# Router selection by pairwise ranks, and a new order of five pieces in the opening of a cross-attention and mixture-of-experts kernel

## What is computed

```python
def xattn(q, k, Wq, Wk, Wv, Wo):            # q = layernorm(x), k = ctx
    sim = einsum('bqd,bkd->bqk', q @ Wq.T, k @ Wk.T)
    sim = (sim - mean(sim, (1, 2))) * rsqrt(var(sim, (1, 2)) + EPS)
    return einsum('bqk,bkd->bqd', softmax(sim), k @ Wv.T) @ Wo.T

def ffn(x):                                 # x = layernorm(x)
    shared = swiglu(x @ sw1 + sb1) @ sw2 + sb2
    probs = softmax(x @ gate_w + gate_b)    # 8 experts
    topk_probs, topk_idx = top_k(probs, 2)
    cw = sum(one_hot(topk_idx, 8) * topk_probs[..., None], axis=2)
    routed = einsum('ebsd,bse->bsd', swiglu(x @ rw1 + rb1) @ rw2 + rb2, cw)
    return shared + routed

x = x + xattn(layernorm(x), ctx, ...)       # x: (8, 256, 128), ctx: (8, 256, 96)
x = x + ffn(layernorm(x), ...)
```

## Time and profile before

| | us |
|---|---|
| median of 3 runs | 155.4 |
| lowest and highest | 154.41, 155.75 |
| the profiled execution | 152.72 |
| its span, first to last instruction | 150.7 |
| TensorE busy | 132.1 (88%) |
| VectorE busy | 108.1 (72%) |
| ScalarE busy | 70.6 (47%) |
| GpSimd busy | 23.7 (16%) |

### The profile page before, as it was taken

The page is one execution under the profiler, slowest core; times in us unless marked ns, Lnnn a source line. Parts: engine busy times, 40 slices in busy tenths (PEclk is TensorE's granted clock), DMA queues, the critical chain, the costliest instruction groups (busy, mean ns, idle before and its releaser), DMA issues.

```text
span 150.7 us, 2018 instructions
## 1 busy us (share of the span) xinstructions
PE 132.1 (88%) x603; PEld 96.5 (64%) x603; DVE 108.1 (72%) x337; ACT 70.6 (47%) x132; POOL 23.7 (16%) x41
## 2 busy tenths in 40 slices
PE   0998894498999999499999998899899989999980
PEld 0786681486878766368778775667576656766740
DVE  3676968486886988974966988829986883865641
ACT  2347955666133127973353129962133783313320
POOL 7083366304020001040200000000300000000000
PEclk9999997558999999999999999999999999999999
DMA  4999000000000000009510000049020008720002
GB/s 127 298 340 255 6 0 7 0 0 2 0 0 4 0 0 2 0 23 325 213 66 8 0 0 0 5 148 382 33 70 0 0 4 229 327 70 7 0 0 72
DMA packets 8493, 11.38 MB, mean 76 GB/s; under 512 B 1265, under 2 KB 6922, under 8 KB 8098
## 3 DMA queue, kind: packets, MB, share of 16 engines
q1 hardware_dynamic: 7906, 11.02, 21.9%
q10 hardware_dynamic: 576, 0.23, 0.6%
HBM read 10.15 MB, written 1.10 MB: 75 GB/s over the span
## 4 chain that ended last, share of the span: by engine, by line
issue 49%; PE 28%; POOL 8%; DVE 6%; ACT 3%; DMA 2%; POOLq 1%; DVEq 0%
PE bank L836 24%; POOL ln_rstd L358 3%; POOL row_powers L349 2%; DMA ctx_sb<-in_ctx_dram 2%; POOL sim_r L364 2%; ACT prob L437 2%; POOL w_rest L371 1%; PE bank L852 1%; POOLq L49 1%; PE bank L844 1%; DVE xn L601 1%; PE bank L995 1%; DVE act L754 0%; DVE silu L746 0%; ACT silu L485 0%
## 5 line engine op out<-in xcount | busy, mean ns | idle before, releaser
L485 ACT ACTIVATE silu<-bank,b_cols 128x512 f32<-128x512 f32 (+1 forms) x37 | 24.9, 676 | 47.2 <-PE bank L836 43.7
L836 PE MATMUL bank<-x_head,w_head 128*128 128x512 f32 x72 | 39.7, 552 | 0.0
L836 PE MATMUL bank<-act,w_sb 128*128 128x512 f32 (+1 forms) x74 | 36.4, 580 | 0.0
L836 PE MATMUL bank<-x_head,w_rest 128*128 128x512 f32 x72 | 28.9, 401 | 0.0
L754 DVE SCALAR_TENSOR_TENSOR act<-bank,b_cols,silu 128x512 f32<-128x512 f32 (+1 forms) x37 | 27.2, 736 | 2.2 <-ACT silu L485 1.4
L836 PE MATMUL bank<-x_rest,w_head 128*128 128x512 f32 x72 | 28.8, 399 | 0.0
L746 DVE TENSOR_TENSOR silu<-silu,cw_all 128x512 f32<-128x512 f32 (+1 forms) x25 | 16.7, 667 | 13.3 <-DMA cw_all<-cw_dram 7.2
L836 PEld LDWEIGHTS bank<-x_head,w_head 128*128 128x128 f32 x72 | 14.0, 195 | 7.6 <-issue 4.6
L836 PEld LDWEIGHTS bank<-x_rest,w_head 128*128 128x128 f32 x72 | 14.1, 195 | 6.7 <-issue 5.2
L836 PEld LDWEIGHTS bank<-act,w_sb 128*128 128x128 f32 x74 | 13.7, 188 | 3.6 <-issue 1.0
L836 PEld LDWEIGHTS bank<-x_head,w_rest 128*128 128x128 f32 x72 | 13.9, 193 | 3.3
(11 more groups left out here) (113 smaller groups left out, 186.1 us busy)
## 6 DMA issues: line engine op xcount, KB each, us to landing
cw_all<-cw_dram SPq DMA_DIRECT2D x3, 1024.0 KB, 6.9
cw_all<-cw_dram SPq DMA_DIRECT2D x6, 256.0 KB, 3.5
cw_all<-cw_dram SPq DMA_DIRECT2D x3, 512.0 KB, 4.9
x_sb<-in_x_dram SPq DMA_DIRECT2D x4, 256.0 KB, 4.0
w_sb<-in_L_ffn_rw_dram SPq DMA_DIRECT2D x1, 1024.0 KB, 7.2
ctx_sb<-in_ctx_dram SPq DMA_DIRECT2D x4, 192.0 KB, 4.1
out_dram<-x SPq DMA_DIRECT2D x3, 256.0 KB, 2.1
w_sb<-in_L_ffn_rw_dram SPq DMA_DIRECT2D x1, 512.0 KB, 7.2
```

What stands on the lines that cost most here:

```text
L485: scalar.activation(silu[:, k, cols], HID[(2 * n) % 3][:, cols], ACT.Silu, bias=b1_cols[:, 0, e:e + 1]).then_inc(silu_sb, 1)
L836: return pe.matmul(dst, lhs, rhs, start=start, stop=stop, skip_group_check=True)
```

## The change

The router's select becomes three instructions on 4 x 8 x 8 elements: the difference of each pair of logits of a token, a comparison with a matrix `tie`, which is `-TINY` where the other expert has the lower index and 0 elsewhere, and a sum over the others. The result, `g_rank`, is the number of experts that come before this one; the mask is `g_rank < 1.5`, taken together with the product with `g_exp` in `router_weights`. GpSimd's constants `tie` (one memset of 64 elements and seven short ones) take the place of `descending` (eight).

In the opening:

- TensorE: `scores_average(0)` stands ahead of `project_u(1)`; `router(c)` takes the groups one after the other, each after its own `x2_head` and `x2_rest`.
- ScalarE: `v_copy(1)` stands behind `prob_copy(0)` and `prob_copy(1)`.
- VectorE: `x2_rests` takes a group; the first group's stands ahead of `scores_scale(1)`, the second's behind it. `router_weights(0)` follows `router_select(0)` directly; `first_statistics(2)` stands behind the gate of expert 0.
- GpSimd: a wait for both `x2_rest` groups ahead of `split_rests(4, 6)`.

```diff
 OPENING = {..., ("project_u", 2), ("u_copies", 2),
+           ("router_weights", 0), ("first_statistics", 2)}
...
     wait_own(pool.memset(powers[:, 1, :], -1.0))
-    for k in range(E):
-        pool.memset(descending[:, k:k + 1], float(E - k)).then_inc(consts_ready, 1)
+    wait_own(pool.memset(tie[:, :, :], 0.0))
+    for e in range(1, E):
+        pool.memset(tie[:, e, 0:e], -TINY).then_inc(consts_ready, 1)
...
     scores_rstd(1)
+    pool.wait_ge(x2_rest_sb, CB)
     split_rests(4, 6)
...
     exponentials(0)
-    v_copy(1)
     prob_copy(0)
     prob_copy(1)
+    v_copy(1)
     split_heads(3, 4)
...
-def x2_rests(c):
-    for g, js in enumerate(groups(c)):
-        cols = batch_cols(js)
...
+def x2_rests(c, g):
+    cols = batch_cols(groups(c)[g])
...
 def router_select(c):
-    for k, left in enumerate((logits, g_left)):
...
-    dve.tensor_tensor(g_mask[:, :, :], g_hot[0][:, :, :], g_hot[1][:, :, :], ALU.add).then_inc(mask_sb, 1)
+    pairs = [P, TC, E, E]
+    own(dve.tensor_tensor(g_diff[:, :, :, :], logits[:, :, :].unsqueeze(2).broadcast_to(pairs),
+                          logits[:, :, :].unsqueeze(3).broadcast_to(pairs), ALU.subtract))
+    wait_own()
+    own(dve.tensor_tensor(g_beats[:, :, :, :], g_diff[:, :, :, :],
+                          tie[:, :, :].unsqueeze(1).broadcast_to(pairs), ALU.is_gt))
+    wait_own()
+    dve.tensor_reduce(g_rank[:, :, :], g_beats[:, :, :, :], X, ALU.add).then_inc(mask_sb, 1)
...
 def router_weights(c):
-    own(dve.tensor_tensor(g_p[:, :, :], g_exp[:, :, :], g_mask[:, :, :], ALU.mult))
+    own(dve.scalar_tensor_tensor(g_p[:, :, :], g_rank[:, :, :], 1.5, g_exp[:, :, :], ALU.is_lt, ALU.mult))
...
     second_normalise(0, 1)
+    x2_rests(0, 0)
     scores_scale(1)
-    x2_rests(0)
+    x2_rests(0, 1)
     router_logits(0)
     router_select(0)
+    router_weights(0)
     dve.wait_ge(setup_sb, 3)
...
     expert_gate(c, e, lambda: run(n, 1))
+    if n == 0:
+        first_statistics(2)
     run(n, 2)
...
 def router(c):
-    pe.wait_ge(x2_head_sb, done(c))
-    pe.wait_ge(x2_rest_sb, done(c))
     if c == 0:
         pe.wait_ge(w_rests, 1)
-    for i in range(TC):
-        for k, xs in enumerate((x2_head, x2_rest)):
+    for g, js in enumerate(groups(c)):
+        pe.wait_ge(x2_head_sb, upto(c, g))
+        pe.wait_ge(x2_rest_sb, upto(c, g))
+        for i in batch_tiles(js):
+            for k, xs in enumerate((x2_head, x2_rest)):
...
     project_v(0)
+    scores_average(0)
     project_u(1)
-    scores_average(0)
     scores(1)
```

More of the change, by code:

```diff
@@ L32 @@
 EPS = 1e-5
+TINY = 2.0 ** -125
 def xattn_moe_kernel(nc, x, ctx, wq, wk, wv, wo, gate_w, gate_b, sw1, sb1, sw2, sb2, rw1, rb1, rw2, rb2, out):
@@ L74, in xattn_moe_kernel @@
         powers = sb("powers", [P, 2, TC])
-        descending = sb("descending", [P, E])
+        tie = sb("tie", [P, E, E])
         pick = sb("pick", [P, E, P], F32R)
@@ L120, in xattn_moe_kernel @@
         g_z, g_exp, g_p = sb("g_z", [P, TC, E]), sb("g_exp", [P, TC, E]), sb("g_p", [P, TC, E])
[L121 to L126, removed]
+        g_best = sb("g_best", [P, TC])
+        g_diff, g_beats = sb("g_diff", [P, TC, E, E]), sb("g_beats", [P, TC, E, E])
+        g_rank = sb("g_rank", [P, TC, E])
         cw_cols = sb("cw_cols", [P, TC, PARTS + 2 * E])
@@ L673, in second_statistics @@
                 ln_variance(1, c, ts)
-            def x2_rests(c):
-                for g, js in enumerate(groups(c)):
-                    cols = batch_cols(js)
-                    dve.wait_ge(x2_head_sb, upto(c, g))
-                    dve.tensor_tensor(x2_rest[:, c, cols], late(c, g)[:, cols], x2_head[:, c, cols].bitcast(F32), ALU.subtract).then_inc(x2_rest_sb, 1)
+            def x2_rests(c, g):
+                cols = batch_cols(groups(c)[g])
+                dve.wait_ge(x2_head_sb, upto(c, g))
+                dve.tensor_tensor(x2_rest[:, c, cols], late(c, g)[:, cols], x2_head[:, c, cols].bitcast(F32), ALU.subtract).then_inc(x2_rest_sb, 1)
             full = [P, TC, E]
@@ L691, in router_logits @@
                 dve.wait_ge(lg_sb, c + 1)
-                own(dve.tensor_reduce(g_best[0][:, :], logits[:, :, :], X, ALU.max))
+                own(dve.tensor_reduce(g_best[:, :], logits[:, :, :], X, ALU.max))
                 wait_own()
@@ L695, in router_logits @@
                     dve.wait_ge(gexp_sb, c)
-                dve.tensor_tensor(g_z[:, :, :], logits[:, :, :], per_token(g_best[0][:, :], full), ALU.subtract).then_inc(gz_sb, 1)
+                dve.tensor_tensor(g_z[:, :, :], logits[:, :, :], per_token(g_best[:, :], full), ALU.subtract).then_inc(gz_sb, 1)
             def router_select(c):
-                for k, left in enumerate((logits, g_left)):
[L701 to L715, removed]
-                dve.tensor_tensor(g_mask[:, :, :], g_hot[0][:, :, :], g_hot[1][:, :, :], ALU.add).then_inc(mask_sb, 1)
+                pairs = [P, TC, E, E]
[6 more added lines that the diff above has]
+                dve.tensor_reduce(g_rank[:, :, :], g_beats[:, :, :, :], X, ALU.add).then_inc(mask_sb, 1)
             def router_weights(c):
```

14 lines of the change are left out of this document (7 added, 7 removed).

## The result

| | before | after |
|---|---|---|
| median, us | 154.91 (4 runs, 153.44 to 155.75) | 148.31 (4 runs, 148.25 to 149.9) |
| profiled execution, us (span) | 152.72 (150.7) | 148.29 (146.1) |
| mean granted clock of it | 0.966 | 0.977 |
| VectorE busy, us | 108.1 | 103.6 |

The ratio is 0.9693, interval 0.9625 to 0.9761. It leaves out executions that lie over 1.5% above the fastest of their kernel, which is why it says less (4.8 us) than the medians do (6.6 us). The two profiled executions differ by 4.6 us of span.

What follows compares the result with a forecast made beforehand. TensorE, 88% busy, was taken as the bound by its stops and slow clock; 2.45 (rests) + 1.15 + 0.1 (select) = 3.7 us off the 155.4 median gave 151.7 us, own range 150.6 to 152.8, with A and B 150.2 to 153.5.

Steps and rivals of the forecast that it cites:

- The rests, 2.45 us: Opening, second layer norm to router: wait, split x2_rests and router matmuls by halves start the first expert matmul 2.45 us earlier.
- The cover of chunk 0's weights: Opening: chunk 0's weights done at 31.4, TensorE wants them at 33.6; 2.2 us of cover, both VectorE moves costed at nothing.
- Average and value copy, 0: Opening, attention: up to 0.9 us gained, but ln_rstd stays behind GpSimd's third w_rest; booked 0 +- 0.25 us.
- The row of 0.13 us: Second layer norm: VectorE's ln_veps was held by GpSimd's subtraction for its last 0.13 us, in agreement with the rule.
- rival A: Opening: ln_veps is not held, so the second half of the layer norm comes 0.7 us earlier: 151.0 us; chance 0.13.
- The select: Router on VectorE: three instructions take 1.35 us instead of 2.42; gains 1.15 us in chunk 1, 0.1 in chunk 3.
- rival D: Select: wide instructions read broadcast patterns slowly; at 1.5 us each the time is 159.2 us; chance 0.03.
- The sum, 3.7 us: Whole kernel: 2.45 + 1.15 + 0.1 = 3.7 us off the profiled execution's 152.7, giving 149.0.
- The median of the runs shown: Last step: the gain taken off the median of 155.4 us, 2.7 above the profiled execution, giving 151.7.
- Rival B: Opening: the clock falls earlier or stays low up to 2.5 us longer, costing 1.25 us: 152.95 us; chance 0.17.

Runs made afterwards that it cites:

- the rests alone: Kernel before with GpSimd's wait, x2_rests in two pieces around scores_scale(1), router matmuls by halves: 150.5 us, ratio 0.9812.
- lower group: The 11 of 39 runs of the unchanged kernel before, in the follow-up experiments, that lie at 152.0 to 152.8 us.
- upper group: The 28 of 39 runs of the unchanged kernel before, in the follow-up experiments, that lie at 154.15 to 155.7 us.
- the subtraction out of the way: Changed kernel with GpSimd's third w_rest subtraction also moved behind the wait for x2_rest: 148.51 us.
- the average and value copy alone: Kernel before with scores_average(0) ahead of project_u(1) and v_copy(1) behind the probability copies: 154.9 us, ratio 1.0129.
- the longest stop: Changed kernel with the select's comparison done four times in chunk 1, TensorE's stop 2.4 us: median 149.92 us, ratio 0.975.
- a stop of 1.8 us: Changed kernel with the select's comparison done three times in chunk 1: 149.79 us, ratio 0.974.
- the weights moved: Changed kernel with router_weights(1) behind the gate of expert 7: 149.01 us, ratio 0.9697.

## Why the prediction was wrong

Point by point, by its own steps:

- **The rests, 2.45 us.** Right in the mechanism, and in the size partly by luck. The first expert matmul is 2.65 earlier in the profile, up to 0.3 of it from the first load, and each of the three parts did what was said. But at half clock a start 2.65 earlier is worth 1.33. The sum carried its 2.45 through whole by taking the clock to be back 2.45 earlier too; it was back 3.7 earlier, and 3.13 were won by step 2. In the profile of the rests alone it was back 1.35 earlier, and 1.63 were won; by the runs 2.1 (lower group) and 1.7 (upper). Undoing the wait alone gave back 0.7 to 0.9 us.
- **The cover of chunk 0's weights.** Right: done at 31.1 (said: 31.4), wanted at 32.95 (said: 33.6); the two moves are worth 0.
- **Average and value copy, 0.** Right in its reason: `ln_veps` was held for 0.6 us and `ln_rstd` starts at 21.63. The row of 0.13 us was not chance, so rival A's condition, that `ln_veps` isn't held, falls. The value of 0 is shown only to within 0.7 us. With the subtraction out of the way the layer norm did come earlier, and the median did not; this price of the half clock was in neither the sum nor rival A.
- **The select.** 1.35 us for three instructions: measured 1.35 (0.42 each). 1.15 us in chunk 1: 1.1 alone, 0.76 in the full change, most of the difference being the 0.25 us of idle VectorE ahead of the gate. 0.1 in chunk 3: 0.15. The wide forms with two broadcast inputs cost what a dense one does, so rival D falls.
- **The sum, 3.7 us.** 3.8 by the last expert, but 0.7 more in the opening and 0.4 less in chunk 1 than the sum had, so the agreement is in part luck. The 0.8 us behind the last stores, which go with the select, were not in it.
- **"The median of the runs shown is 155.4 and lies 2.7 us above the profiled execution; I take the gain off it."** This is the step that failed. I took the 2.7 us as something both kernels would have. By the profiles they are TensorE's clock: 1.65 us for the half clock behind the stop for expert 7's `silu`, in the executions where it falls there, and about 1 us for a late opening. The profiled execution was one without either. The change cuts the stop from 2.0 to 1.2 us, and in none of the ten runs of the changed kernel does the second low stretch show in the mean clock. The right sum would have set 149.0 against executions like the profiled one (measured 148.3 to 148.6; the difference is about the 0.8 at the end) and not added the surplus. The part that is a late opening could have stayed, since the changed kernel has such executions too; why its median shows, by its time, none is not explained.
- **Rival B** had the clock as the thing that could go otherwise, but only in the opening and only as a loss. In the opening it went the other way: the low stretch lasts 6.8 us in the changed kernel's profile and 10.2 in that of before. That a shorter stop could win more than its own length is what I did not think of, though I had both rows: a stop of 2.0 us on TensorE, and a spread of the runs.

What stays open: why the upper group has 28 of 39 runs of before, 6 of 6 with the average and value copy alone, 3 of 7 with the rests alone and 2 of 6 with the longest stop. With a stop of 1.8 us or less no profile has the second low stretch; two runs without GpSimd's wait, at 150.0 and 150.5 with mean clocks of 0.962 and 0.961, were not profiled and leave it possible there. Open too are the 0.25 us ahead of the gate, what makes an opening late, and which instruction gives the 0.8 us behind the last stores.

## What to carry over

Before a gain worked out in one trace is taken off a median, ask which executions the median is made of: if the profiled one is faster than nearly all runs, something is missing from it, and the mean clocks of the runs are the first place to look. The one stop of TensorE of about 2 us in this kernel cost more than its length in a part of the executions, so it was worth shortening ahead of shorter ones. A start that moves inside a stretch of half clock is booked at half, and the return of the clock as a term of its own. And a GpSimd instruction on two SBUF tensors is best placed where VectorE has neither two-input work nor a `tensor_scalar` like `ln_veps`: letting the one of 1.8 us go behind `row_scale` gave 0.7 to 0.9 us here, for one wait.

## What the hardware showed that I had not expected

- The second low stretch behind one stop: 1.65 us for a stop of 2.0 us, and none for 1.8 us in six runs.
- Starting work earlier under a low clock gives half of the shift, and the clock's return the rest of the account: 2.65 us of start and a return 3.7 earlier became 3.13 by step 2, 1.4 and 0.4 became 0.9, and 0.66 with a return 0.3 later became 0.2.
- Executions of one order of instructions with an early and a late opening, 1.2 to 1.7 us apart at step 2 in the changed kernel and its variants, whose mean granted clock can be the same (0.977).
- 0.25 us of idle VectorE at about one place of its stream, ahead of the gate in the changed kernel and ahead of `cw_cols` with the weights moved, absent where `router_weights(0)` stands in its old place. With the comparison repeated it is absent (three times) or 0.1 to 0.2 us (four times). No row explains it.
